# Constant products on TensorE in the opening of the two pair attentions

## The reference

```
x = x + L0_cross_attention(norm(x), ctx);  x = x + L0_ffn(norm(x))
x = x + L1_cross_attention(ctx, ctx, norm(x), mask)     # 16 heads of 8
x = x + L1_ffn(norm(x))
x = x + L2_cross_attention(norm(x), ctx)                # 16 heads of 64
x = x + L2_ffn(norm(x))                                 # a local transformer
x = x + L3_cross_attention(norm(x), ctx, ctx, bias)     # 16 heads of 8
x = x + L3_ffn(norm(x))

L1, L3:  q, k, v = projections;  s = q k^T (scaled; L1 masked, L3 plus a bias for each key)
         out = softmax(s) v, heads joined, times Wo, plus bo
```

## Time and profile before

| | us |
|---|---|
| median of 3 runs | 1659.95 |
| lowest and highest | 1658.11, 1660.13 |
| the profiled execution | 1655.33 |
| its span, first to last instruction | 1653.5 |

### The profile page before, as it was taken

How to read it: one execution, slowest core, us unless ns; L and a number is a source line. 1 busy time by engine, 2 the same in 40 slices (tenths; PEclk the granted TensorE clock), 3 DMA queues, 4 the chain that set the end, 5 groups by cost and what they waited for, 6 DMA issues and landing times. The chain is left out here.

```text
span 1653.5 us, 52545 instructions
## 1 busy us (share of the span) xinstructions
PE 1431.4 (87%) x21230; PEld 770.0 (47%) x21230; DVE 1266.6 (77%) x3493; ACT 990.3 (60%) x2154; POOL 541.4 (33%) x618
## 2 busy tenths in 40 slices
PE   5885999998667999999999788889888878999975
PEld 3631343443433555545555555655565542333333
DVE  4636688884888878787878769967699757898848
ACT  2330566666856666575666278853788513777764
POOL 1215565640110000000000279915799123434100
PEclk9985899999778999999999989999899986999997
DMA  5123434320110000000000000010200003232100
GB/s 161 30 38 95 122 81 89 83 47 2 52 41 1 3 9 9 3 9 10 30 3 3 2 9 1 0 52 1 52 1 0 17 16 87 42 55 39 30 2 26
DMA packets 61584, 55.97 MB, mean 34 GB/s; under 512 B 9866, under 2 KB 53054, under 8 KB 61382
## 3 DMA queue, kind: packets, MB, share of 16 engines
q1 hardware_dynamic: 60518, 52.74, 13.4%
q10 hardware_dynamic: 864, 0.39, 0.1%
HBM read 29.91 MB, written 1.05 MB: 19 GB/s over the span
## 5 line engine op out<-in xcount | busy, mean ns | idle before, releaser
L1968 ACT ACTIVATE probs_l2x<-probs_l2x,nmax_l2x 128x512 f32<-128x512 f32 x256 | 182.7, 715 | 153.9 <-DVE nmax_l2x L1838 153.6
L1838 DVE CUSTOM_DVE_ANT_0 probs_l2x<-s_ps_l2x,mask_b_l2x 128x512 f32<-128x512 f32 x248 | 161.1, 686 | 85.9 <-PE s_ps_l2x L2047 84.2
L1089 DVE CUSTOM_DVE_ANT_0 junk_l1x<-s_ps_l1x,mask_b_l1x 128x512 bf16<-128x512 f32 x256 | 166.2, 686 | 44.7 <-PE s_ps_l1x L1294 42.8
L1092 DVE TENSOR_REDUCE nmax_l3x<-s_ps_l3x 128x1 f32<-128x512 f32 x256 | 163.8, 683 | 32.4 <-PE s_ps_l3x L1294 30.6
L1151 ACT ACTIVATE pT_l1x<-st_ps_l1x 128x1024 f32<-128x1024 f32 x128 | 131.2, 1025 | 72.0 <-PE st_ps_l1x L1279 72.0
L1850 DVE STREAM_TRANSPOSE pT_l2x<-probs_l2x 128x512 f32<-128x512 f32 x256 | 166.3, 687 | 0.0
L2047 PE MATMUL s_ps_l2x<-kT_l2x_first,q_l2x 64*32 64x512 f32 x1984 | 136.8, 608 | 11.6 <-DVE nmax_l2x L1838 10.7
L2603 POOL TENSOR_TENSOR v_l2x_first<-kT_l2x_first,tb_l2a_first 128x256 f32<-128x256 f32 x112 | 118.8, 1086 | 30.3 <-ACT kT_l2x_first L2754 30.3
L2063 PE MATMUL pv_ps_l2x<-pT_l2x,v_l2x_first 32*64 32x256 f32 x4096 | 124.0, 383 | 3.5 <-issue 3.5
L2063 PEld LDWEIGHTS pv_ps_l2x<-pT_l2x,v_l2x_first 32*64 32x64 f32 x4096 | 91.3, 132 | 39.1 <-issue 14.7
L1781 POOL TENSOR_TENSOR spread_l2x<-inv_l2x,consts 128x512 f32<-128x512 f32 x16 | 17.6, 1100 | 266.6 <-DVE inv_l2x L1857 266.6
(11 more groups left out here) (531 smaller groups left out, 3429.7 us busy)
## 6 DMA issues: line engine op xcount, KB each, us to landing
mask_i_l1x<-in_mask SPq DMA_DIRECT2D x8, 512.0 KB, 4.8
maskT_i_l1x<-in_mask_t SPq DMA_DIRECT2D x8, 512.0 KB, 5.1
kT_l1x_first<-parts_l1x_first SPq DMA_DIRECT2D x60, 64.0 KB
kT_l3x_first<-parts_l3x_first SPq DMA_DIRECT2D x60, 64.0 KB
q_l1x<-parts_l1x_first SPq DMA_DIRECT2D x90, 32.0 KB
q_l3x<-parts_l3x_first SPq DMA_DIRECT2D x90, 32.0 KB
ctxT_l0x<-in_ctxT SPq DMA_DIRECT2D x9, 256.0 KB, 3.3
rows_l0x<-in_ctx SPq DMA_DIRECT2D x9, 256.0 KB, 4.2
```

What stands on the lines that cost most here:

```text
L1089: dve.tensor_tensor_reduce(out=junk[w][:], in0=s_ps[w][:], in1=mask_b[b % 2][:, j, :], scale=-1.0, scalar=3e38, op0=ALU.add, op1=ALU.min, ...
L1092: dve.tensor_reduce(to, s_ps[w][:], AX.X, ALU.max, negate=True).then_inc(m.s_drained[w].sem, 1)
L1838: dve.tensor_tensor_reduce(out=probs[n % 4][:], in0=score_bank(b, s, w), in1=mask_b[b % 2][:], scale=-1.0, scalar=3e38, op0=ALU.add, op1=A ...
L1968: act.activation(probs[n % 4][:], probs[n % 4][:], ACT.Exp, bias=nmax[:, b % 2, n:n + 1], scale=-1.0, accum_out=sums[:, r, w, qb:qb + 1]). ...
```

## The change

A 256-column part of the second transposed-score bank gets a name, and constant products are written to it: 28 of them (14 in L3) between the output bias product and the first scores, and one behind each score product of the steps t < 0, so 28 more in each attention.

```
         misc = psum(m, ctx, f"misc_{tag}", [P, 512])
+        idle_ps = st_ps[1][:, 1, 0:256]
...
                     pe.matmul(misc[:, 0:D], bv_all[:], wo_s[:], start=False, stop=True).then_inc(m.bo_turned.sem, 1)
+                stay_awake(m, pe, idle_ps, 14 if biased else 28)
                 for t in range(-LEAD, LAST_SLOT + 1):
                     for j in range(2):
                         if masked and 0 <= t < T:
...
                         for w in range(2):
                             if t + LEAD < T:
                                 scores(t + LEAD, j, (w,))
+                            if t < 0:
+                                stay_awake(m, pe, idle_ps, 1)
                             if 0 <= t < T:
                                 transposed_scores(t, j, (1 - w,))
```

## The result

The changed kernel takes 1670.22 us (median; 1666.14 to 1673.51), the kernel before 1657.11 us on the same chip (1652.09 to 1660.13): a ratio of 1.0082 with a 95% interval of 1.0061 to 1.0103, about 13 us slower. The forecast was 1657.7, with 1652.0 to 1662.3 as its range. The profiled execution spans 1671.4 us, 17.9 more than before; it is the slowest of the change's six timed executions, 3.3 us above their median. Every line number is one to four higher.

A forecast was written before the change was run, and what follows sets the result against it. The prediction took the low 1.2 GHz TensorE clock to bind from step 0 on, and the opening's end to hang on the transfer behind Q(1). L1 -1.15 and L3 -1.1 make -2.25 us against 1659.95: 1657.7, range 1652.0 to 1662.3.

The forecast's parts named there:

- At the low clock a half then needs 2 x (427 + 213) = 1280 ns of streaming: Steps t < 0: two scores and two constant products fit the 1400 ns period of a half, 120 ns left.
- The sum's 0.65 us: L1's opening: exposed products behind scores delay Q(1), so the mask and step 0, by 0.65 us.
- its 0: L3's opening: the same 0.65 us delay only eats the slack of 0.7 us, so it costs 0.
- rival 3: Openings: PE becomes the bound, a half needs 1680 ns, 3.9 us lost per attention, 1667 us in all; chance 0.10.
- Cost 0 ahead of the scores: Before the first scores: 28 or 14 products hide in PE's wait for the transfer, at least 2.4 and 1.5 us left.
- Q(1) 4.7 us behind the first score: Openings: Q(1) was expected to start 4.7 us behind the first score, where it had been 4.06.
- step 0 after 25.4: L1: step 0 was expected to start 25.4 us behind the first score, where it had been 24.8.
- The end is set by the transfer behind Q(1): Opening's end: step 0 ends on the mask transfer following Q(1); faster scores between them buy almost nothing.
- over 1.5: Sign in the openings: the maxima's period would exceed 1.5 us if PE became the bound, against 1.40 before.
- L3's slack of 0.7 us: L3's opening: the moved maxima were taken to land 0.7 us, between 0 and 1.84, ahead of step 0.
- The clock at 1.00 by step 0, half of 3.6 and 2.2 us won: Behind step 0: full clock by about step 0 in both attentions, gaining 1.8 us in L1, 1.1 in L3.
- Behind the openings a lead or a loss is kept, 1.5 us either way: Later stages: nothing changes and a lead is kept, with 1.5 us allowed for the clock's later falls.

The follow-up runs named there:

- e3: The change, but each product behind a score takes 64 rows, those the score does not use; 1659.13 us, ratio 1.0021 to the kernel before.
- e4: The change, but each product behind a score takes the same 64 rows as that score; 1659.79 us in a single execution.
- e5: The change with 128 columns in place of 256 in each product behind a score; 1668.97 us in a single execution.
- e1: The change with only the products ahead of the first scores, none behind the scores; 1657.57 us, ratio 1.0005 to the kernel before.
- e2: The change with only the products behind the scores, none ahead of the first scores; 1669.28 us, ratio 1.0084 to the kernel before.
- e11: The kernel before plus 56 products of 8 columns ahead of L1's first scores, nothing else; 1664.71 us, ratio 1.0055 to the kernel before.
- e16: The kernel before plus 104 products of 8 columns ahead of L1's first scores, nothing else; 1654.79 us, ratio 0.9986 to the kernel before.
- e12: The change plus 48 products of 8 columns ahead of L1's first scores; 1663.26 us, ratio 1.0032 to the kernel before.
- e10: The kernel before plus extra DVE maxima in L1's opening, no constant products; 1663.17 us, ratio 1.0035 to the kernel before.
- e7: The change in L1's pair attention only, L3 as before; 1668.23 us, ratio 1.0071 to the kernel before.

## Why the prediction was wrong

**The step that failed** is "At the low clock a half then needs 2 x (427 + 213) = 1280 ns of streaming (...) it fits, with 120 ns left". The term for the changes between the operands stood at zero. It measured 0.11 us, four times a half: 1280 + 440 = 1720 ns against 1.73 us in the trace. 14 x (1.73 - 1.40) = 4.6 us of the 4.9 that L1's opening lost; e3 and e4, which take it away, and e5, which leaves it whole with half the streaming, show the term. The sum's 0.65 us was 4.9 in L1, and its 0 was 4.1 in L3.

The error was in the reading of the earlier trace rows: 12 products with the same full-array weights, one behind the other, hide their loads (the change's own 28 ahead do so too, 5.03 us in all at 136.93), and I took that for a score between two of them. It was rival 3, at a chance of 0.10, that described what came, its price of 0.10 us included (1680 ns a half, 3.9 us per attention). The rule of the Trainium skill that stood behind the sum (TensorE: Matmul & The Clock Gate, Part 3: Packing small matmuls, "The mechanism") was right for this alternation. Its load of 128 columns, 107 ns by the formula of that page of the Trainium skill (Part 2, LDWEIGHTS), is 0.11 us here, and the half of 1.71 us estimated from it is 1.73. For e3's disjoint rows the case agrees with it too. For e4 the Trainium skill's sentence that a load overlaps only where the row groups differ does not hold: there the rows of score and product overlap, and the load is hidden all the same, so the measurement decides.

**Point by point.** *Cost 0 ahead of the scores*: right, 3.41 us of cover left, e1 within 0.2 %. *Q(1) 4.7 us behind the first score*: it was 5.5; *step 0 after 25.4*: it was 29.7. *The end is set by the transfer behind Q(1)*: right before, wrong after; PE became the bound, as the text's list of signs has it ("over 1.5" for a maxima's period). *L3's slack of 0.7 us*: not borne out. L3 lost 0.8 less than L1, but its first four scores ran at the full clock; in e2, where they did not (0.50 from 1362.5 to 1403.5), L3 lost 5.5 us, 0.6 more than L1. *The clock at 1.00 by step 0, half of 3.6 and 2.2 us won*: it came up 3.1 us behind L1's step 0 and fell again 3.4 us later. The gain that the prediction put at 2.9 us is 0.9 in L1 and 0.1 in L3 from the first exponential to the ninth, no more than the kernel before varies by. *Behind the openings a lead or a loss is kept, 1.5 us either way*: wrong by 4 to 6 us. This was the second failure, and no step or rival named it. e11 shows that the count of instructions is enough for it, e16 and e12 that another count undoes it, e10 that a delay does not make it. That the forecast's rival 3, at 1667 us, came near the measured 1670 is in part luck: its 7.1 us stand against 9.0 in the openings, and the rest came from a cause that it did not have.

**The account.** 9.0 us in the openings, 3.3 to 6.0 in the local stage (408.1 against 402.1 to 404.8 in three profiles of before), less 1 in L1's exponentials: 11 to 14, where 13 were measured. All of these but the 13 are of single executions, and the change's second profile has 411.6 in the local stage. The profiled execution's other 4 us are its later start of L1's scores (1.3) and pieces under 1 us each, which I leave to scatter. One thing does not fit well: e2 lost 13.9 us by its ratio with openings of +4.9 and +5.5 and a local stage of 402.8; its interval reaches down to 9.4.

**What stays open.** That PE waits for its next block of instructions is argued from the time order, not shown by an edit of the fetch. Why e3, e7 and the change's second execution have a stage of 411.6 to 411.7 us and e4, e5, e11 and the change's first one of about 408 shows in the clock: two stretches of 6.8 us at 0.50 behind such pauses, not one. In e3 and the change's second execution the further one follows a pause of 1.8 and 2.1 us near 988 us, in e7 one of 2.1 us at 1220.28. The change's second execution:

```profile
989.30:996.10 6.80, 6.42 (x116) 4.21 (x115) 6.50 (x16) 3.68 (x15) 5.38 (x6) 0.50 0.02 6
```

e4, e5 and e11 have that first pause too, of 1.5 us (it ends at 982.81, 991.88 and 988.69), and their clock stays at 1.00. Why a pause brings the clock down in one execution and not in another is open.

## What to carry to other kernels

Before putting cheap filler between two products, ask whether it makes the array change its rows, and price each change at one weight load against the slack of the loop. It was 0.11 us here at 1.2 GHz, and 0.10 to 0.11 at 2.4 GHz as well (the first scores of L3 in the change, 0.31 and 0.22 us apart from the constant products, where streaming takes 0.21 and 0.11). Filler of 64 rows cost the opening under 0.5 us, on the half of the score ahead of it as on the other. A row of like products one behind the other says nothing on unlike ones in turns. And when a change moves time in a stage that it does not touch, count the instructions ahead of that stage, and try the edit's count alone with tiny products before looking for a cause in the work.

## What the runs showed of the hardware

A run of PE products stopped here for 0.8 to 2.3 us with no releaser, at a place that moved with the number of instructions ahead; in the nine cases given it went on 2.3 to 2.9 us behind the start of a 16 KiB instruction packet. At these places PE issued fast: 124 products with their 125 weight loads in 1.7 us (1002.56 in e11), less than that delay. The Trainium skill (Runtime: NRT & Kernel Launch, Instruction fetch mechanics) has such blocks hold 256 instructions and calls the cost of crossing one mostly hidden; at most of the 25 packets of before's local stage the trace agrees, and at these places it does not. 56 tiny products cost 0.55% of the kernel [0.33, 0.76], and 48 more gave it back.

And the clock: ten microseconds with PE busy 10.00 of 10.00 and a full-array product behind each score stayed at 0.50, as 8.34 of 10 had the earlier trace rows.
